# One-pass softplus sums, time-step units ahead of the projections, and two exponent products on GpSimd, in an early-fusion kernel

## The reference

```python
u  = x @ W_x.T + b_x;   g = sigmoid(x @ W_g.T + b_g)          # x = layernorm(h0), 2176 rows
h  = depthwise_conv3(u) + conv_b                              # mixed with u by the gate g
dt = softplus(x @ W_dt.T + b_dt)                              # (32, 68, 512)
dt = clip(mean of dt over batch and position, 0.001, 2.0)     # one value a channel
A_bar = exp(dt * A);  K[k] = sum_s C * B_bar * A_bar**k       # k = 0..67, 16 states
y  = causal convolution of h with K, then @ W_out.T           # then layernorm and experts
```

## Time and profile before

| | |
|---|---|
| median of 3 runs | 497.0 us (496.97 to 497.46) |
| span of the profiled execution, first to last instruction | 495.2 us |
| what lies around the span, against the median | 1.8 us |
| busy PE / DVE / ACT / POOL | 442.5 / 330.5 / 296.4 / 152.2 us |
| mean granted clock of TensorE | 0.967 |

### The profile page before, as it was taken

One profiled execution on the slowest core, in us unless ns is written; L12 is line 12 of the kernel. 1 busy time (PEld: TensorE's weight loads), 2 busy tenths in 40 slices (PEclk: granted clock), 3 DMA queues, 4 the chain that ended last, 5 costly groups with the idle time before them and its releaser, 6 DMA issues.

```text
span 495.2 us, 9980 instructions
## 1 busy us (share of the span) xinstructions
PE 442.5 (89%) x3149; PEld 363.4 (73%) x3149; DVE 330.5 (67%) x980; ACT 296.4 (60%) x667; POOL 152.2 (31%) x255
## 2 busy tenths in 40 slices
PE   8989989799899999999999798999999999999400
PEld 5769967667778878887777577888878888888300
DVE  6885567678999434335786777866674666666584
ACT  2854359177975465316554354887786777877341
POOL 2000000000000000001243887874778644543322
PEclk9999999799999999999999999999999999999955
DMA  7981089900019942972511222232322333252262
GB/s 178 187 228 56 33 253 322 292 0 2 1 35 259 217 114 58 228 228 81 180 54 52 89 94 77 86 97 66 107 98 76 107 107 110 74 155 69 78 213 82
DMA packets 58734, 59.94 MB, mean 121 GB/s; under 512 B 25368, under 2 KB 51260, under 8 KB 57404
## 3 DMA queue, kind: packets, MB, share of 16 engines
q1 hardware_dynamic: 54236, 48.68, 36.4%
q0 software_dynamic: 3552, 9.74, 5.3%
q10 hardware_dynamic: 896, 0.89, 0.6%
HBM read 34.50 MB, written 24.80 MB: 120 GB/s over the span
## 4 chain that ended last, share of the span: by engine, by line
PE 66%; DVE 12%; issue 7%; ACT 7%; POOL 4%; DMA 2%; SPq 1%; DVEq 0%; POOLq 0%; ACTq 0%
PE bank L1040 14%; PE bank L881 9%; PE bank L433 8%; PE bank L435 8%; PE bank L434 8%; PE bank L955 3%; PE bank L1030 3%; PE bank L901 3%; POOL sorted_x L671 2%; PE bank L1012 2%; ACT U L470 1%; DVE spj L1400 1%; DMA got<-expert_y 1%; PE bank L848 1%; PE bank L947 1%
## 5 line engine op out<-in xcount | busy, mean ns | idle before, releaser
L1040 PE MATMUL bank<-w,hr 128*128 x320 | 76.0, 380 | 1.5 <-DVE ysb L1661 1.5
L1040 PEld LDWEIGHTS bank<-w,hr 128*128 128x128 f32 x320 | 60.1, 190 | 11.7 <-issue 2.7
L644 POOL MEMSET ones<- 2x128 f32 x1 | 0.2, 194 | 212.3 <-PE bank L916 212.3
L1234 ACT ACTIVATE hr<-bank,gsel 128x128 f32<-128x128 f32 x160 | 59.9, 460 | 0.2 <-PE bank L1030 0.2
L719 POOL DMA_INDIRECT expert_y<-ysb,toid x40 | 42.8, 1071 | 51.3 <-DVE ysb L1661 34.7
L881 PE MATMUL bank<-Tb,U 68*32 68x68 f32 x1024 | 45.9, 358 | 0.3 <-issue 0.3
L881 PEld LDWEIGHTS bank<-Tb,U 68*32 68x32 f32 x1024 | 40.6, 139 | 3.6 <-issue 3.1
L1646 DVE BATCH_NORM_STATS2 bsth<-bank 128x6 f32<-128x512 f32 x40 | 27.7, 693 | 20.5 <-PE bank L435 20.2
L671 POOL DMA_INDIRECT sorted_x<-x2s,slot x34 | 33.8, 994 | 15.3 <-issue 9.2
L1226 ACT ACTIVATE hn<-bank,nmrh,rsh 128x512 f32<-128x512 f32 x40 | 31.1, 777 | 10.0 <-DVE nmrh L1655 8.1
L433 PE MATMUL bank<-w_hi,bT_hi 128*128 x80 | 35.0, 438 | 0.1
(11 more groups left out here) (297 smaller groups left out, 1153.3 us busy)
## 6 DMA issues: line engine op xcount, KB each, us to landing
Tb<-ssm_kernels SPq DMA_DIRECT2D x16, 680.0 KB, 7.5
sorted_x<-zpad SPq DMA_DIRECT2D x6, 1419.0 KB, 13.6
xg<-sorted_x SPq DMA_DIRECT2D x40, 129.0 KB, 2.1
got<-expert_y SPq DMA_DIRECT2D x17, 256.0 KB, 3.6
XI<-in_x_dram SPq DMA_DIRECT2D x12, 288.0 KB, 5.6
h0r<-h_spill SPq DMA_DIRECT2D x17, 128.0 KB, 2.1
out_dram<-acc SPq DMA_DIRECT2D x17, 128.0 KB
w1raw<-in_L_ffn_w_dram SPq DMA_DIRECT2D x4, 512.0 KB, 15.9
```

What stands on the lines that cost most here:

```text
L1040: mm = pe.matmul(bank[6][:, 0:D], hr[:, i % 3, c, :], w2[:, bass.ds(expert[i], 1), c, :].rearrange("p o n -> p (o n)"), start=(c == 0), st ...
L1234: last = act.activation(hr[:, i % 3, c, :], bank[3 + i % 2][:, c * P:(c + 1) * P], ACT.Relu, scale=gsel[:, i, 0, c:c + 1], bias=gsel[:, i, ...
```

## The change

- `capped(q)` now adds the bias, takes the smaller of the sum and a tile `cap` of 40s, and sums the capped values into `dtm`. The bank is free after this one pass. `taken` is gone. The Ln on ACT sums its output (`accum_out` into `dts`).
- What the cap cut off is put back as a sum: N times the bias plus the sum of the uncapped products, less the sum of the capped values (`over`). The sum of the products comes from two extra columns of `xT`, made of `xsum`, the sum of all rows, which POOL adds up tile by tile and PE turns with two matmuls.
- All 20 units come before the projections of group 0, in block order 3, 0, 1, 2, 4. The 34 unused matmuls are gone. Group 0 is projected all u first, then all g.
- POOL makes `Eb` products 2 and 3, DVE 0 and 1. ACT takes u parts of group 0 between the exponentials, and the gates of group 0 after them.
- DVE mixes group 0 after the kernel sums; its copy of `kt` stands after the first block of it. In `C_STEPS`, kT comes after three blocks of group 1, turns(0) after all of group 1, and ssm 0 to 3 before the projections of group 2.

```diff
-        BLOCK_ORDER = [3, 4, 0, 1, 2]
+        BLOCK_ORDER = [3, 0, 1, 2, 4]
...
-        C_STEPS = (proj(1, range(NB)) + turns(0) + [("kT",)] + proj(2, range(NB)) + ssm(0, 4) + turns(1)
+        KT_AT = 3
+        POOL_POWERS = 2
+        C_STEPS = (proj(1, range(KT_AT)) + [("kT",)] + proj(1, range(KT_AT, NB)) + turns(0) + ssm(0, 4) + proj(2, range(NB))
...
-            act.activation(spt[:, q % 4, 0:w], spt[:, q % 4, 0:w], ACT.Ln, bias=onec[:]).then_inc(sem("dt_ln"), 1)
+            act.activation(spt[:, q % 4, 0:w], spt[:, q % 4, 0:w], ACT.Ln, bias=onec[:],
+                           accum_out=dts[:, q % HC, q // HC:q // HC + 1]).then_inc(sem("dt_ln"), 1)
...
+            for m in range(NT):
+                pool.wait_ge(sem("x"), m + 1)
...
+                    pool.tensor_tensor(xsum[:], xsum[:], xs[:, m % 2, :], ALU.add).then_inc(sem("on_pool"), 1)
...
+            for j in range(POOL_POWERS, HC):
+                pool.tensor_tensor(Eb[:, j], adt[:, j].rearrange("p (o s) -> p o s", o=1).broadcast_to([P, L, S]),
...
-            for q in range(2, AHEAD):
+            for q in range(2, HC * NB):
                 project_dt(q)
-            for nb in range(NB):
-                pe.wait_ge(sem("xT"), ready_tiles(nb))
-                project(0, nb)
-            pe.wait_ge(sem("v_init"), 4)
-            idle(bank[1], 20)
-            for q in range(AHEAD, HC * NB):
-                project_dt(q)
+            for kinds in "ug":
+                for nb in range(NB):
+                    project(0, nb, kinds)
...
-                    idle(bank[4], 14)
...
+            u_parts(0, 0)
             act.wait_ge(sem("adt"), 1)
             act.activation(wmix[:], adt[:], ACT.Exp).then_inc(sem("a_exp"), 1)
-            u_parts(1, 0)
-            u_parts(1, 1)
             for j in range(HC):
-                act.wait_ge(sem("adt"), j + 2)
+                if j < POOL_POWERS:
+                    act.wait_ge(sem("adt"), j + 2)
+                else:
+                    act.wait_ge(sem("on_pool"), NT + j - POOL_POWERS + 1)
                 act.activation(Eb[:, j], Eb[:, j], ACT.Exp).then_inc(sem("powers"), 1)
+                u_parts(0, j + 1)
+            for nb in range(NB):
+                gate(0, nb)
...
             def capped(q):
...
-                dve.tensor_scalar(spt[:, q % 4, 0:w], bank[4 + q % 4][:, 0:w], vec[:, bdt0 + j:bdt0 + j + 1], 40.0,
-                                  ALU.add, ALU.min).then_inc(sem("dt_capped"), 1)
...
+                if q >= 4:
+                    dve.wait_ge(sem("dt_ln"), q - 3)
...
+                dve.scalar_tensor_tensor(spt[:, q % 4, 0:w], bank[4 + q % 4][:, 0:w], vec[:, bdt0 + j:bdt0 + j + 1],
+                                         cap[:, 0:w].bitcast(F32), ALU.add, ALU.min,
+                                         accum_out=dtm[:, j, k:k + 1]).then_inc(sem("dt_read"), 1)
...
             for j in range(HC):
                 kernel_sum(j)
+            for nb in range(NB):
+                convolve(0, nb)
+                if nb == 0:
+                    q = C_RING.index(("kT",))
+                    dve.wait_ge(sem("c_ps"), q + 1)
```

More of the change, by code:

```diff
@@ L227, in build_kernel @@
         ones2, ebk = place(R6 + size(H), R7, ("ones2", [2, P], F32R), ("ebk", [P, NK]))
-        (busy,) = place(R6, R7, ("busy", [P, 512], F32R))
+        (cap,) = place(R6, R7, ("cap", [P, 512], F32R))
+        CAP = 40.0
         (Kk,) = place(R6, TOP, ("Kk", [P, HC, L]))
@@ L593, in _ @@
         def _(pool):
-            pool.memset(busy[:].bitcast(F32), 1.0).then_inc(sem("busy"), 1)
+            pool.memset(cap[:].bitcast(F32), CAP).then_inc(sem("cap"), 1)
             pool.memset(ident[:], 0.0).then_inc(sem("ident"), 1)
@@ L743, in warm @@
                 for _ in range(count):
-                    pe.matmul(ps[:], busy[:, 0:P], busy[:], start=True, stop=True)
-            pe.wait_ge(sem("busy"), 1)
+                    pe.matmul(ps[:], cap[:, 0:P], cap[:], start=True, stop=True)
+            pe.wait_ge(sem("cap"), 1)
             warm(bank[0], 16)
@@ L1114, in gate @@
                                scale=-1.0).then_inc(sem("gate"), 1)
[L1116 to L1127, removed]
+            act.preload_act_table_set("natural_log_exp_and_others")
+            for q in range(HC * NB):
+                w = BLOCKS[BLOCK_ORDER[q // HC]][1]
+                act.wait_ge(sem("dt_read"), q + 1)
+                act.activation(spt[:, q % 4, 0:w], spt[:, q % 4, 0:w], ACT.Exp).then_inc(sem("dt_exp"), 1)
+                if q > 0:
+                    log1p(act, q - 1)
+            log1p(act, HC * NB - 1)
             act.wait_ge(sem("conv_consts"), 6)
[L1129 to L1133, removed]
+            u_parts(0, 0)
             act.wait_ge(sem("adt"), 1)
             act.activation(wmix[:], adt[:], ACT.Exp).then_inc(sem("a_exp"), 1)
[L1137 to L1138 removed]
             for j in range(HC):
[L1140 removed]
+                if j < POOL_POWERS:
+                    act.wait_ge(sem("adt"), j + 2)
+                else:
+                    act.wait_ge(sem("on_pool"), NT + j - POOL_POWERS + 1)
                 act.activation(Eb[:, j], Eb[:, j], ACT.Exp).then_inc(sem("powers"), 1)
+                u_parts(0, j + 1)
+            for nb in range(NB):
+                gate(0, nb)
             for step in C_STEPS:
@@ new lines, in _ @@
+            dve.wait_ge(sem("xsum_mm"), 1)
+            column = lambda t: t[:, :, N:NX]
+            sums = bank[3][:, 0:DC].rearrange("p (c o) -> p c o", o=1).broadcast_to([P, DC, NX - N])
+            signal(dve.tensor_copy(column(xT_hi), sums), "xsum_in", 1)
+            dve.tensor_tensor(column(xT_lo), sums, column(xT_hi).bitcast(F32), ALU.subtract).then_inc(sem("xsum_in"), 1)
+            dve.wait_ge(sem("a_exp"), 2)
+            link(dve.tensor_tensor(amat[:], araw[:], atmp[:], ALU.max))
@@ L1425, in _ @@
+            link(dve.tensor_scalar(amat[:], amat[:], -1.0, None, ALU.mult))
+            link(dve.tensor_scalar(winv[:], amat[:], 1e-6, None, ALU.add))
+            link(dve.reciprocal(winv[:], winv[:]))
+            for q in range(HC + 1, HC * NB):
+                capped(q)
             dve.wait_ge(sem("dt_read"), HC * NB)
+            link(dve.reduce_sum(over[:], dtm[:, :, 0:NB], AX))
+            link(dve.scalar_tensor_tensor(over[:], vec[:, bdt0:bdt0 + HC], float(N), over[:], ALU.mult, ALU.subtract))
@@ L1426, in _ @@
+            link(dve.tensor_tensor(over[:], over[:], dtm[:, :, NB], ALU.add))
+            dve.wait_ge(sem("dt_ln"), HC * NB)
             link(dve.reduce_sum(dt1[:], dts[:], AX))
+            link(dve.tensor_tensor(dt1[:], dt1[:], over[:], ALU.add))
             link(dve.tensor_scalar(dtc[:], dt1[:], 1.0 / N, 0.001, ALU.mult, ALU.max))
@@ L1435, in _ @@
             dve.wait_ge(sem("consts"), 6)
-            for j in range(HC):
+            for j in range(POOL_POWERS):
                 dve.tensor_tensor(Eb[:, j], adt[:, j].rearrange("p (o s) -> p o s", o=1).broadcast_to([P, L, S]),
```

102 lines of the change are left out of this document (43 added, 59 removed).

## The result

The changed kernel takes 498.85 us (median of 20 runs, 497.4 to 500.7) against 497.5 (median of 20, 495.8 to 500.4) for the kernel before, measured beside it: ratio 1.0027, 95% interval 1.0015 to 1.004. It is slower, by about 1.3 us. Forecast were 0.5 us less. The profiled executions point the same way, with spans of 497.0 and 495.2 us.

A forecast was written before the change was run, and what follows sets the result against it. PE was taken to set the pace. The end point moved from 157.4 to 155.7 (-1.7), plus 1.2 for low clock: -0.5. Span 494.7 with 1.8 around it gave 496.5 us, range 493.3 to 500.0.

The forecast's parts named there:

- dear sum: Rival, ACT's Ln: the sum costs up to 0.38 us a unit, last Ln 3.8 us later, 500.3 us; chance 0.14.
- The sum in ACT's Ln: Units: summing the Ln's output adds 0.19 us a unit on ACT, so the last Ln ends at 94.9.
- cheap sum: Rival, ACT's Ln: the accumulator read hides, below 0.16 us a unit; 3 us sooner, 493.5 us; chance 0.33.
- The floor of 91.9: Units: earliest end of the last Ln, PE's end at 90.6 plus a short unit's DVE and ACT passes.
- Part 2: From the sum to the kernels: `adt` at 96.0, first exponential 97.3, gate done 107.8, kernel sums end at 109.3.
- POOL is too slow: Rival, exponent products: beyond 4.0 us each on POOL, the last exponential and gates wait; at 5 us 498.5; chance 0.06.
- the ledger's end point: Units, groups 0 to 2, turns(0), kT and ssm 0 to 3 done: 157.4 before, 155.7 forecast, plus 1.2 for clock.
- DVE's stand before `kt`: After block 0 is mixed by 112.3, DVE waits for kT, holding the other mixes and turns(0): 7 to 8 us.
- PE idle: Ahead of turns(0): PE finishes group 1 at 124.0 and waits 8 us, until 132.0.
- the clock stays low: Rival: g0.2 and group 1 at half pace, +2.5, 499.0 us; or ssm 0 and 1, +1.3; chance 0.13.
- the forecast wait of 2.3 us: Group 0: after two g blocks PE waits 2.3 us for the first gate.
- three signs of being wrong: DVE not standing before `kt`, POOL's products taking over 4 us, or PE waiting anew after 157.

The follow-up runs named there:

- the run with the late copy: The changed kernel with DVE's copy of `kt` behind the third mixed block of group 0 instead of the first: 494.03 us, ratio 0.9913.
- the fill: The changed kernel with 34 unused matmuls added in PE's idle time ahead of turns(0): 499.23 us, ratio 1.0033.

## Why the prediction was wrong

The direction was wrong: -0.5 us forecast, +1.3 measured. The sum held each edit in its place and one price was missing. The measured 498.85 lies inside the range of 493.3 to 500.0, but by luck: the range reached so far for a dear sum and a low clock. Measured beside forecast, in us from the start of the span:

- **The sum in ACT's Ln.** Taken at 0.19, bounds 0 and 0.38. The read takes 0.18 but the next instruction starts 0.09 behind it, so 0.09 is its price, which is inside the condition of the rival *cheap sum*. It is also what the estimate from the Trainium skill (ScalarE: Activation LUTs, What ACT_TABLE_LOAD costs) gave. Right mechanism, oversized term: the last Ln's read ends at 93.98, forecast 94.9. The floor of 91.9 was not reached: through the full units PE's unit of 1.39 us was the bound, and from 89.59 on ACT worked without a gap through what was left, longer than the one short unit that the floor assumed.
- **Products and the first exponential: the step that failed.** Part 2 says "The first product is 4.90 / 4 = 1.22, so ACT's first exponential starts at 97.3." With `adt` 0.9 sooner it should then have been 96.4. It was 98.41, because the product took 3.04: it had to let POOL's 2.04 pass. The rival *POOL is too slow* asked only when POOL's results come and ACT asks for them. They came in time, 2.54 each for 2.8 assumed and 4.0 allowed; the cost was in what POOL took from DVE. I let a neighbour lengthen POOL's instruction and left DVE's at the price without one. Taken out, this term gives back 1.7 us of the median and 2.4 us at kT. The Trainium skill, GPSIMD Engine Reference, Key points, which I cited beside that rival, names DVE instructions with two SBUF inputs; the prediction even wrote that DVE's products are such, and put no price on it.
- **The rest of the sum, read from the run with all products on DVE.** Its marks are nearly those of the forecast: first gate 106.46 for 107.1, kT ends at 119.87 for 119.9, turns at 131.74 for 132.0, state-space steps at 139.19 for 138.0 and 1.2 of clock. Part of this is luck, since `adt` came 0.9 us early there too and PE took 0.6 longer from the first gate to kT. At the ledger's end point the run is at 157.4, level with the kernel before and not 0.5 ahead; its median, 0.6 us less, has an interval that includes no change. So the missing price accounts for the miss, but that the rest of the change gains 0.5 us is not shown.
- **First gate** forecast at 107.1, measured 108.98. **kT** ends at 122.2, forecast 119.9. **Turns** at 134.10, forecast 132.0. **State-space steps** at 141.41, forecast 138.0 and 1.2 of clock. The shift stays near 2 us: everything behind the products is one chain, and nothing of it was absorbed.
- **DVE's stand before `kt`** 7 to 8 us, measured 7.35; **PE idle** 8, measured 7.79. This was right, and the run with the late copy showed it to be worth 4.8 us.
- **The clock.** It fell behind the 8 us of idle, as forecast, and the turns took 6.63 us for 5.4, my 1.2. (That the turns wait for ACT in half their time was a guess: the waits between them before sum to 1.0 of 5.4 us.) It also fell behind the waits in group 0, which the prediction had as the rival *the clock stays low*: 0.54 in 101 to 108 us. That cost nothing there, because the matmuls end about when the first gate frees the bank: PE goes on at 109.72 without the forecast wait of 2.3 us, and from there at full clock. Three runs with or without unused matmuls show no gain in the median from keeping the clock up.
- **The end point** 159.8 for 156.9. Of these 2.9 us some 2.1 are there at the turns; the rest is 5.85 for 5.3 us in the first state-space steps, at full clock, and 0.2 in group 2. I can't explain the slower steps.
- **Behind 157 us** I expected the difference to pass on whole. It was 3.0 us at the start of the last 512 state-space matmuls (201.89 for 198.91), and these with group 3's turns took 26.99 us for 28.45, so about half came back. It goes in part with a gap of 0.4 us among group 3's turns, which only the kernel before has, and for the rest with the pitch of the state-space matmuls, which differs between stretches (5.2 to 6.0 us for 128) in both kernels; why stays open.
- **Two smaller slips.** The prediction says that some 20 us of the stretch are not work of the result; its own terms, 4.6, 3.2, 4.4 and 2.5, sum to 14.7. The sum did not use it. And none of its three signs of being wrong came (DVE stood, POOL's products took 2.54 us, PE did not wait anew behind 157): what DVE's own products would take was not on the list.

Shown by experiment are the exclusion of POOL and DVE (three runs in which POOL's work lay in three places), the price of DVE's stand, and that the two add. Why a low clock costs so little is shown for the kernel before, by the run without its unused matmuls, and for the first gate; for the turns it stays open, as one execution with the fill gained 1.5 us there and the median nothing. Not explained are the projections' pitch, 0.232 us for about 0.228 (rows that begin at no multiple of 32 bytes are excluded), and that of the state-space matmuls.

## What to carry to other kernels

Before work goes from DVE to GpSimd, look at what DVE does beside it: if those instructions read two tensors from SBUF, the engines take turns, so let GpSimd's lie beside reductions (shown here only with spare products between multiplies, not as a gain). Price an offloaded instruction on both engines: when its result is wanted, and whom it keeps waiting meanwhile. In a queue that carries a path, a copy which waits for another engine belongs on an engine with slack; here, with all products on DVE, it was worth 9.8 us (497.16 to 487.37), more than the 7.8 us of unused matmuls that the change removed.

## What the chip showed that I had not expected

- DVE's product of 64 elements a partition took 1.95 us instead of 0.23 beside POOL's product of 1088, and one of 1088 took 3.03 to 3.16 instead of 1.22 to 1.28. A reduction of 1088 elements beside it took 1.29, no more than alone, and ACT's exponential 1.11, as without POOL.
- POOL's product of 1088 elements takes 2.04 us when it has the way, 1.67 times DVE's 1.22. Two on each engine took 95.19 to 101.42 = 6.2 us, about 2 x (2.04 + 1.2) = 6.5; four on DVE 4.90.
- With the clock kept up at one wait it fell at the next, in the one execution profiled of each: 1.00 for 0.72 in 96 to 108 us, then 0.91 for 1.00 in 108 to 126.
